# One table of positions for the pieces of a software-pipelined delta-rule step

## The reference

```python
h = layernorm(x) * (1 + ca) + sa
x = x + ga * attention(h)        # gated delta rule, 32 heads, DK 48, DV 96, then a small dense net
h = layernorm(x) * (1 + cb) + sb
x = x + gb * experts(h)          # top 2 of 8 experts and a shared one
```

```python
S = S * exp(g_t); mem = k_t @ S
S = S + outer(k_t, (v_t - mem) * beta_t); o_t = (q_t * scale) @ S
```

## Time and profile before

| | |
|---|---|
| median of the runs | 2745.7 us |
| the profiled execution's own time | 2746.2 us |
| its span | 2744.4 us |
| PE busy | 2481.4 us (90%) |
| DVE busy | 2036.6 us (74%) |
| ACT busy | 1703.8 us (62%) |
| POOL busy | 886.6 us (32%) |

### The profile page before, as it was taken

How to read it: one execution, slowest core, us unless ns; L and a number is a source line. 1 busy time by engine, 2 the same in 40 slices (tenths; PEclk the granted TensorE clock), 3 DMA queues, 4 the chain that set the end, 5 groups by cost and what they waited for, 6 DMA issues and landing times. The chain is left out here.

```text
span 2744.4 us, 59594 instructions
## 1 busy us (share of the span) xinstructions
PE 2481.4 (90%) x21984; PEld 2058.6 (75%) x21984; DVE 2036.6 (74%) x4303; ACT 1703.8 (62%) x3890; POOL 886.6 (32%) x1053
## 2 busy tenths in 40 slices
PE   1279999999999999999999999999999999889997
PEld 0168888888888888888888888888888888646655
DVE  3478888888888888888888888888888888534444
ACT  1157777777777777777777777777777777512221
POOL 0033333333333333333333333333333333200000
PEclk6599999999999999999999999999999999989998
DMA  2321121112111211121111211021111111031000
GB/s 94 96 54 38 35 55 38 40 38 57 38 40 40 57 40 40 40 57 40 40 40 43 54 40 40 26 69 36 35 36 56 39 39 26 5 116 31 17 14 16
DMA packets 148317, 120.45 MB, mean 44 GB/s; under 512 B 24305, under 2 KB 128698, under 8 KB 148034
## 3 DMA queue, kind: packets, MB, share of 16 engines
q1 hardware_dynamic: 148034, 116.66, 15.9%
HBM read 72.11 MB, written 2.54 MB: 27 GB/s over the span
## 5 line engine op out<-in xcount | busy, mean ns | idle before, releaser
L743 DVE TENSOR_TENSOR dr_w<-dr_ps,mask 128x512 bf16<-128x512 f32 x768 | 526.6, 686 | 250.2 <-PE dr_ps L559 250.2
L757 DVE SCALAR_TENSOR_TENSOR dr_y<-dr_ps,dr_cw,dr_y 128x255 f32<-128x255 f32 (+2 forms) x1152 | 481.3, 473 | 21.1 <-ACT dr_y L873 19.1
L859 ACT CAST dr_tn<-dr_ps 128x512 bf16<-128x512 f32 x640 | 375.6, 587 | 177.7 <-PE dr_ps L572 175.2
L862 ACT CAST dr_tt<-dr_ps 128x512 bf16<-128x512 f32 x768 | 460.4, 599 | 1.2 <-PE dr_ps L579 1.2
L656 PE MATMUL dr_ps<-dr_w,dr_am 128*128 128x96 f32 x3072 | 417.4, 279 | 2.5 <-ACT dr_w L919 2.5
L656 PEld LDWEIGHTS dr_ps<-dr_w,dr_am 128*128 128x128 f32 x3072 | 377.8, 192 | 10.6 <-ACT dr_w L919 3.0
L579 PE MATMUL dr_ps<-dr_tt,dr_w 128*128 128x128 bf16 x3072 | 297.5, 219 | 52.2 <-DVE dr_w L743 52.2
L999 POOL TENSOR_TENSOR dr_fo<-dr_vo,dr_nhalf 128x4 f32<-128x4 f32 x128 | 130.2, 1017 | 652.8 <-DVE dr_vo L828 652.8
L559 PE MATMUL dr_ps<-dr_tn,dr_b 128*128 128x128 bf16 x3072 | 296.8, 219 | 0.0
L572 PEld LDWEIGHTS dr_ps<-dr_w,dr_tt 128*128 128x128 bf16 x2560 | 186.9, 100 | 130.2 <-issue 69.7
L873 ACT ACTIVATE dr_y<-dr_ps,dr_cw 128x256 f32<-128x256 f32 x384 | 160.9, 470 | 184.9 <-PE dr_ps L596 184.9
(11 more groups left out here) (188 smaller groups left out, 4721.4 us busy)
## 6 DMA issues: line engine op xcount, KB each, us to landing
dr_abc<-scr_a SPq DMA_DIRECT2D x64, 512.0 KB, 5.6
dr_qk<-dr_sy SPq DMA_DIRECT2D x384, 48.0 KB, 2.0
dr_hb<-hT SPq DMA_DIRECT2D x64, 256.0 KB, 2.5
dr_bcb<-scr_b SPq DMA_DIRECT2D x128, 64.0 KB, 4.7
dr_qk<-dr_sy SPq DMA_DIRECT2D x128, 32.0 KB, 1.9
ex_modb<-scr_mod SPq DMA_DIRECT2D x4, 1024.0 KB, 7.8
dr_wo<-in_Wo SPq DMA_DIRECT2D x1, 3072.0 KB, 11.0
dr_wv<-in_Wv SPq DMA_DIRECT2D x8, 384.0 KB, 4.2
```

Of the source, the lines that this page charges most:

```text
L743: v.tensor_tensor((tn if l == 0 else w16)[:, us, :], ps[:, (X0, X1)[g], :].rearrange("p (u n) -> p u n", u=QH), bc(mask[:, l, :], 1, QH), ...
L757: v.scalar_tensor_tensor(y[:, slot, x:T], ps[:, BANK[n], off:off + T - x], cw[:, t, TAPS - 1 - x:TAPS - x], y[:, slot, x:T], ALU.mult, ALU ...
L859: act.copy(tn[:, us, :], ps[:, (X2, X1)[g], :].rearrange("p (u n) -> p u n", u=QH)).then_inc(s["tn_ok"], 1)
L862: act.copy(dst, ps[:, (X0, X2)[g], :].rearrange("p (u n) -> p u n", u=QH)).then_inc(s["tt_ok"], 1)
```

## The change

The four tables and the half slots are replaced by one table PLAN. It gives each of the 82 pieces a position, a real number in turns of length 15. The whole part of position / 15 is the stage (0 to 3), and the rest is the place within the turn. In each turn the pieces are issued in the order of this rest. No instruction, buffer or semaphore is added or taken away, and every piece still issues the same instructions on each engine. Only the order changes.

```diff
+PLAN = ((0.44, ("proj", 0)), (1.01, ("taps", 0, 0)), (2.07, ("proj", 1)), (2.47, ("taps", 0, 1)),
+        (2.7, ("taps", 1, 0)), (3.16, ("taps", 1, 1)), (3.21, ("silu", 0)), (3.39, ("proj", 2)), (3.46, ("silu", 1)),
+        (3.68, ("taps", 2, 0)), (5.11, ("norms",)), (5.36, ("taps", 2, 1)), (5.68, ("gains",)), (6.07, ("silu", 2)),
+        (6.31, ("gate", 0)), (6.54, ("decays", 0)), (7.11, ("gate", 1)), (7.41, ("keys",)), (8.72, ("scores", 0)),
+        (8.74, ("decayed", 0, 0)), (9.21, ("decayed", 0, 1)), (10.66, ("decays", 1)), (10.83, ("values", 0)),
+        (12.03, ("scores", 1)), (12.56, ("decayed", 1, 0)), (12.85, ("negate", 0)), (12.89, ("round", 0)),
+        (13.19, ("decayed", 1, 1)), (13.41, ("values", 1)), (13.71, ("negate", 1)), (14.39, ("merge1", 0, 0)),
+        (15.76, ("merge2", 0, 0)), (15.82, ("merge1", 0, 1)), (16.35, ("merge2", 0, 1)), (16.83, ("merge1", 1, 0)),
...
+        (19.25, ("keys_scale",)), (20.19, ("merge2", 2, 0)), (20.37, ("merge1", 2, 1)), (20.47, ("merge2", 2, 1)),
...
+        (27.0, ("merge1", 6, 0)), (28.06, ("merge2", 6, 0)), (28.09, ("merge1", 6, 1)), (29.65, ("merge2", 6, 1)),
+        (30.22, ("w0", 0)), (31.2, ("residual", 0, 0)), (32.11, ("delta", 0, 0)), (33.17, ("residual", 0, 1)),
+        (34.72, ("delta", 0, 1)), (35.44, ("state_out",)), (36.21, ("ks",)), (36.87, ("w0", 1)),
+        (37.07, ("mean", 0)), (37.33, ("residual", 1, 0)), (38.05, ("gated", 0)), (38.56, ("delta", 1, 0)),
+        (39.12, ("oT", 0)), (39.37, ("residual", 1, 1)), (40.05, ("wo", 0)), (41.56, ("acc", 0)),
+        (42.76, ("delta", 1, 1)), (43.94, ("out", 1)), (44.58, ("mean", 1)), (46.93, ("gated", 1)),
+        (48.08, ("oT", 1)), (49.63, ("wo", 1)), (49.9, ("acc", 1)))
...
+        TURN = sorted((x % SLOTS, int(x // SLOTS), piece) for x, piece in PLAN)
...
+        def slots(stages, on):
+
+            for _, k, piece in TURN:
+                if stages[k]:
+                    on[piece[0]](stages[k], *piece[1:])
```

More of the change, by code:

```diff
@@ L422, in delta_rule @@
         block = ctx.enter_context(nc.Block())
[L430 to L440, removed]
@@ L443, in delta_rule @@
[L443 to L447, removed]
@@ L448, in delta_rule @@
[L448 to L466, removed]
+        SLOTS = 15
@@ L468, in run, with steps @@
+        DEPTH = 4
+        TURN = sorted((x % SLOTS, int(x // SLOTS), piece) for x, piece in PLAN)
+        def steps(turn):
+            for i in range(STEPS + DEPTH - 1):
+                turn([(i - k, (i - k) % NB) if 0 <= i - k < STEPS else None for k in range(DEPTH)])
+        def slots(stages, on):
+            for _, k, piece in TURN:
+                if stages[k]:
+                    on[piece[0]](stages[k], *piece[1:])
         def run(eng, on):
-            steps(eng, lambda a, b, c, d: slots(a, b, c, d, on))
+            steps(lambda stages: slots(stages, on))
```

## The result

The changed kernel takes 2634.3 us, the median of four runs (2630.9 to 2636.1). The kernel before took 2746.8 in the runs beside it. The ratio is 0.9588, with a 95% interval of 0.9571 to 0.9604: faster by 113 us. Forecast were 2653 us and a range of 2625 to 2695.

A forecast was written before the change was run, and what follows sets the result against it. PE bounds the kernel: a 35.02 us step is 32.95 of matmuls plus 2.07 of holes. With 0.55 of new holes, 33.50, a gain of 1.52; 61 times gives 93, so 2746.2 - 93 = 2653 us, range 2625 to 2695.

The forecast's parts named there:

- the three old holes: PE waits before `merge2` 6,1 (0.97 us), `merge1` 0,1 (0.34) and `gate` 0 (0.76); all go, removing 2.07 a step.
- The price of new holes: Waits on PE made by the new order: 0.55 us a step as nearest, bounds 0 to 1.6.
- `residual` 0,1 behind the copy of w: On PE: ACT's copy of w stands behind two evictions of `proj` 1, a new hole of 0.32 us.
- `oT` 0 behind POOL: On PE: `mean` 0 now comes behind `gains` in POOL's queue, so `oT` 0 waits 0.23 us.
- the collision: `decays` 0's scan on DVE meets POOL's second `dg`: charged 0.76 us on DVE and 0.92 on POOL each step.
- `merge2` 0,1: On PE: its mask starts 0.45 us after `merge1` 0,1 and lasts 0.69, a new hole of 0.06.
- the ramp: Turns without all four stages, bound by chains of waits: zero change taken, 4 us either way.
- the most likely stretch: The forecast's own case: step 33.2 to 34.0 us, 2632 to 2683 us, chance 0.66.
- POOL keeps the port: Rival: scan on DVE also waits behind POOL's second `dg` and the power; step 35.0, 2746 us, chance 0.03.
- the same, through `kqb`: Rival: scan waits until both `kqb` are done; step 36.4, 2831 us; chance 0.04 with other waits over 1.5 us.
- A slower outcome: Kernel slower through `kqb` or another wait of over 1.5 us, chance 0.04.

The follow-up runs named there:

- the late taps: New table with `taps` 2,1 moved from 5.36 to 6.25, behind `ks` and ahead of `gate` 0, and `silu` 2 to 6.26: 2791.2 us, ratio 1.015 to the kernel before.
- the two hand edits: Old tables with `out` 1 and `mean` 1 one half slot later: 2906.4 us; the same with `mean` 0 also later: 2908.4 us.
- the hand edits of the old tables: Old tables with `out` 1, `mean` 1 later: ratio 1.057; `mean` 0 later: 0.9861; all three: 1.058; these plus `gated` 1, `oT` 1, `wo` 1 later: 0.9929.
- the old tables' first edit: Old tables with `out` 1 moved from half slot 12 to 13 and `mean` 1 from 13 to 14: 2906.4 us, ratio 1.057 to the kernel before.
- the edit of both: Old tables with `out` 1, `mean` 1 and `mean` 0 each one half slot later: 2908.4 us, ratio 1.058 to the kernel before.

## Why the prediction was right, and where it was off

**The bound and the three old holes: shown.** That a step is PE's work plus holes of 0.97, 0.34 and 0.76 us holds for both ends. Each hole is gone in the profile after. Each comes back when its cause alone is restored: 0.95 by `merge2` 6,1, 1.86 by POOL's order, 1.98 by the late taps (the last two are larger than the old ones, since the pieces around stand otherwise in the new order: `mean` 1 comes later, and `gate` 0 directly behind `ks`). The third was also closed alone in the old tables, for 0.66 us a step. PE's work of 32.95 us was right to 0.12: with no hole left, the step is 32.83. The 0.1 that the prediction had set aside is in it, a group that is slow when it comes behind a hole: `gate` 0 took 1.40 behind its hole (1498.96 to 1500.36) and takes 1.29 now (1001.74 to 1003.03).

**The price of new holes: the mechanism right, the size off.** The term was 0.55 us a step over 32.95, the profile after shows 0.27 over it (0.39 over the 32.83 of a step with no hole, 0.1 of which is the slow `residual` 0,1). Of its three parts:
1. `residual` 0,1 behind the copy of w: forecast 0.32, measured 0.29, and gone when the evictions are put behind the copy. Shown.
2. `oT` 0 behind POOL: forecast 0.23, measured none. The chain was right: the product ends at 1008.94, that is 7.94 us after `gam` (1001.00), where I had 8.0, and the collision with its 2.55 is in it. Two starts were off: `gam` ends 0.19 after `merge1` 3,0's start and not 0.34, and PE takes 8.91 us to `oT` 0 and not 8.7. `og` is ready at 1009.53, PE comes at 1009.72. Two errors of 0.15 to 0.2 us in the layout turned a hole of 0.23 into a cover. That this hole is missing is the layout's error and not its merit.
3. `merge2` 0,1, 0.06: measured 0.03. It starts 0.95 behind `residual` 0,0 (1020.49 to 1021.44) instead of 0.92.

The 0.28 us less in a step are 17 of the 19 us between forecast and measurement. The rest is in the ramp: the first three distances are 2.6 us shorter together, where the forecast had one step's 1.5 in them, and 1.6 us of the span lie outside the distances. One sum is off: by 61 steps, the lower end of the most likely stretch (33.2 us) is 2635 us and not 2632.

**"POOL keeps the port" and "the same, through `kqb`": not what happened.** Their place and partner were right, since the scan is stretched to 1.78 in 56 of the 57 steps between 250 and 2150 us (1.64 in the other). But it ended before the power in each of them, and the mask of `merge1` 3,1 was in time. The price was wrong as well: in the kernel with the late taps the power runs first, and the scan starts half a microsecond into it without being held, and so in every step but the first:

```profile
1212.52 1.64 POOL L972 TENSOR_TENSOR dr_nrm<-dr_kk,dr_half 128x8 f32<-128x8 f32 x1
```

```profile
1213.03 1.21 DVE L766 TENSOR_TENSOR_SCAN dr_dec<-dr_abc,dr_dg 128x512 f32<-128x512 f32 x1
```

So a running power would not have cost the scan the 1.63 us that I gave it, but the first half microsecond at most, which no run shows. The Trainium skill's rule (SBUF — State Buffer, Who interferes with whom), that the one that starts first blocks the other fully, is borne out here by the large products and the scan, and not by this power over 8 elements, which takes 1.64 us and lets the scan run through most of it.

**A slower outcome** had its chance at the wrong place. What makes such a table slower is seen in the two hand edits: a chain over POOL of which some members stay behind, and the clock that follows a hole of two microseconds. I had priced a hole only at its own length, which was enough for the 0.97, 0.76 and 0.34 us of the kernel before, behind which the clock stayed, and not for two microseconds.

## What to carry to other kernels

When one engine is nearly full, read the distances between its starts, not its busy share: the excess over the same instruction's usual distance is the list of holes, and their sum, with about 0.1 us for the slow group behind a hole, is the whole that an order can give. For each hole ask what could stand in the gap, and then what that filler was covering where it stood before: the hand edits of the old tables came out between 1.4% better and 5.8% worse. Where one table orders all engines, a piece may have to be split, so that on one engine a copy passes two evictions without moving anything on the others.

## What the hardware showed that I had not expected

- The clock behind a hole. After idle stretches of 0.97 us on PE no full step of before shows it fall. After 1.86 us it fell 17 times of 56 in one kernel, and cost 1.61 us when it did; after 1.98 us, 12 of 56. After 1.96 us in the old tables' first edit it fell 34 times of 53, and the granted clock was 0.67 on the mean of the next 3.4 us; in the edit of both, the same hole was followed by a fall 53 times of 53. So the length of the hole alone doesn't decide, and what does isn't settled by these runs.
- The exclusion of DVE and POOL is by instruction, in either direction: a scan of 1.22 took 1.78 behind a product, and the power behind that scan 2.55 instead of 1.64; two `kqb` of 1.41 took 2.40 behind a scan. A power already 0.51 us under way did not hold up a scan (1.22).
- The first matmul group behind even a short hole is slow: `residual` 0,1 takes 0.97 us behind 0.29 of waiting, and 0.87 without it.
